# Making 22 contexts' keys and values one layer early, in a decoder of four layers

## The chip, the cores and the metric

One core of a Trainium2 chip runs the kernel. The metric is the device time of one launch in microseconds (us), the median of several runs. TensorE (PE) multiplies matrices and turns tiles over, writing to PSUM; VectorE (DVE), ScalarE (ACT) and GpSimd (POOL) work on vectors; SyncE (SP) issues most of the transfers between DRAM and SBUF. Each engine runs its own instructions in order and waits for others on semaphores.

## The reference

The input x is 32 sequences of 32 tokens of 256 numbers; the context is 32 sets of 257 rows of 256. Four layers follow each other, and each has a cross attention to the context, a self attention and a feed-forward part, all added to x. What the change touches most is the cross attention of layer 1, with 16 query heads of 64 and a single head of keys and values:

```
xn = layer_norm(x, ln_g, ln_b)
cn = layer_norm(context, cln_g, cln_b)
q = (xn @ Wq) in 16 heads * scale
k, v = halves of cn @ Wkv               # one head, 64 + 64 wide
sim = einsum('bhid,bjd->bhij', q, k)
out = einsum('bhij,bjd->bhid', softmax(sim), v) @ Wo
h, gate = halves of xn @ Wff1
out = out + silu(gate) * h @ Wff2
```

Layer 0's feed-forward part, which stands before it, sends each token to the nearest of 8 experts, `a * silu(g) @ down[e]` with `a, g` the halves of `xn @ up[e]`.

## The kernel before

x stays in SBUF (`core.X`, 8 tiles of 128 tokens). Each part of a layer is a function with one block per engine, and the order of instructions on each engine is written out by hand. Two areas `core.weights[0]` and `[1]` hold a part's weights in turn; `load_weights` fills the next layer's while one works (`pack3` are the weights of layer 1's cross attention, `pack4` those of its self attention).

*Layer 0's experts* (`l0_feed_forward`): POOL scales the rows (L2115), PE and DVE find each token's expert (`router_tensor`, `ex.places`), SP stores the rows in DRAM and loads three experts. Then POOL adds the skip part to X (L2119) and issues gathers of sorted rows (L1062 in `move_rows`). PE runs filler matmuls (`keep_busy`, L91) while it waits: 10 before the tokens are found, 8 before the first gather has landed, 28 behind the loop over 15 groups. `up` is L1113, `down` L1124.

*Layer 1's cross attention* (`l1_cross`): the context's mean and spread come from tiles that SP loads in four slots (`ContextNorm.load`), with DVE taking statistics (L1391, L1396). The layer norm of the context is folded in: the weights get cln_g and lose their mean (`scaled_kv`, `centred_kv`: L2272 on POOL, L2287 on PE, L2482 on DVE), and each context's keys and values are scaled with its spread afterwards. PE makes queries (L2302), the feed-forward's up (L2323) and down (L2384), and then turns over 32 contexts:

- `sim(b+1)`: scores of the next context, L2349, in PSUM banks 0 to 3. The odd heads' keys come from a copy in the other 64 partitions (`kT_odd`), which SP moves.
- `flip_probs(b)`: weights turned over, L2360.
- `keys_values(b+3)`: L2332, reads `ctxT` from DRAM; to bank 6.
- `weigh(b)`: L2376, reads the copied flipped weights.
- `flip_values(b+3)`: L2338, reads `kvT`.

DVE in one turn: tops of b+1 (L2519), its half of the copy of flipped weights of b (L2530), reciprocal of the first half's sums (L2524), `scale_keys_values(b+3)` (L2505, PSUM times the row of spreads), second reciprocal, `copy_values(b+3)` (L2513). ACT: its half of the copy (L2456), four exponentials (L2448), output copy (L2461). POOL multiplies the weights with the reciprocals (L2278), twice a turn.

At each border the norm of X follows: `take` gathers statistics of a pair of tiles, `early_vector` and `early_scalar` norm the first half of the tiles while the rest is being made, and PE flips them (L308).

Of the kernel before, what the change touches and what calls it, by code (L numbers as in the profile page):

```python
# [18 lines left out]
P = 128  # L19
# [15 lines left out]
class Core:  # L35


    def __init__(self, nc, es, dram):
# [33 lines left out]
        self.left = self.sem("left")  # L72
        self.norm = Norm(self)
# [84 lines left out]

def load_weights(core, sp, layer):

    w, mem = core.dram[f"pack{layer}"], core.weights[layer % 2]
    at = after_slots(layer)
    sp.dma_start(mem[:, at:at + w.shape[1]], w).then_inc(core.weights_in[layer], 16)
# [31 lines left out]
class Norm:  # L195
# [11 lines left out]
    def take(self, dve, written, tiles):  # L207

        c, nc = self.core, self.core.nc
        if written is not None:  # L210
            c.dve_step(dve, written)
        for t in tiles:
            done = nc.vector.bn_stats(c.stats[:, t, :], c.X[:, t, :])
# [142 lines left out]
class SelfAttention:  # L356
# [77 lines left out]
    def project_tensor(self, pe, xT, wqk, wv):  # L434
# [3 lines left out]
        self.project(pe, xT, xT, wqk, wv, (0, 1))  # L438
        flip.tensor(pe, 1)
        self.project(pe, xT, xT, wqk, wv, (2, 3))  # L440
# [31 lines left out]
    def copy_projections(self, act, side_of, squares=None, size=None, second_half=None, values_from=0, **root):  # L472
# [7 lines left out]
        for t in range(NT):  # L480
# [12 lines left out]
            if t == 1 and second_half is not None:  # L493
                second_half()
# [415 lines left out]
RING = 3  # L910

# [10 lines left out]
class SortedExperts:  # L922
# [10 lines left out]
    def __init__(self, core, es, name, layer, kind, choices, shared=False):  # L933
# [33 lines left out]
        if shared:  # L967
            self.slots = [sb("slot0", [P, width + extra])[:], mem[:, width:2 * width + extra], sb("slot2", [P, width + extra])[:]]
        else:
            whole = width + extra  # L970
            self.slots = [sb("slot0", [P, whole])[:], mem[:, whole:2 * whole], mem[:, 0:whole]]
# [81 lines left out]
    def move_rows(self, pool):  # L1053
# [17 lines left out]
        for i in range(RING):  # L1071
            gather(i)
        pool.wait_ge(places.targets_found, 1)
# [135 lines left out]
    def vector(self, dve, between=lambda n: None, final=False):  # L1209
# [51 lines left out]
        self.over(dve, lambda: None, turn, lambda: copy_out(*divmod(self.N - 1, RING), False), steps=4 if self.kind == "swiglu" else 0)  # L1261
        for g in range(NT // 2):
# [10 lines left out]
            else:  # L1273
                self.core.norm.take(dve, done, tiles)
                if g == 2:
                    self.core.norm.early_vector(dve)
# [171 lines left out]
def l0_cross(core, load_next):  # L1448
# [22 lines left out]
    with ExitStack() as es:  # L1471
# [95 lines left out]
        def _(pe):  # L1567
# [174 lines left out]
            core.keep_busy(0, 4)  # L1742

        @block.scalar
        def _(act):
# [115 lines left out]
            norm.roots(act, 0, 0)  # L1861
            out_squares(3, 7)
            norm.rows_by_scalar(act, 0, 0)

        @block.vector
        def _(dve):
# [148 lines left out]
            for pair, bank in enumerate((2, 3, 6, 7)):  # L2015
                norm.take(dve, add_out(pair, bank), (2 * pair, 2 * pair + 1))
                if pair == 2:
                    norm.early_vector(dve)


def l0_self(core, load_next):
# [5 lines left out]
    with ExitStack() as es:  # L2027
# [9 lines left out]
        def _(sp):  # L2037
            core.enter(sp)
            load_next(sp)

        @block.tensor
        def _(pe):
            flip.tensor(pe, 0, idle=(4, 2, 2))
# [21 lines left out]
        def _(dve):  # L2065
# [4 lines left out]
            for t in range(NT + 1):  # L2070
# [4 lines left out]
                if t == 1:  # L2075
# [7 lines left out]
def l0_feed_forward(core, load_next):  # L2083
# [5 lines left out]
    with ExitStack() as es:  # L2089
        ex = SortedExperts(core, es, "l0f", 2, "glu", 1)  # L2090
# [9 lines left out]
        gate_done = core.sem("l0f_gate_done")  # L2100
        block = core.block

        @block.sync
        def _(sp):
            core.enter(sp)
            load_next(sp)
# [3 lines left out]
        def _(pool):  # L2110
            pool.wait_ge(core.weights_in[2], 16)
# [5 lines left out]
            pool.wait_ge(skips_done, 1)  # L2117
            for t in range(NT):
                done = nc.gpsimd.tensor_scalar(core.X[:, t, :], core.X[:, t, :], more[:, t:t + 1], less[:, t:t + 1], ALU.mult, ALU.add)  # L2119
            done.then_inc(skipped, 1)  # L2120
            ex.move_rows(pool)

        @block.tensor
        def _(pe):
            flip.tensor(pe, 0, idle=(4, 1, 2))
            flip.tensor(pe, 1, idle=(4, 0, 3))
            core.enter(pe)
            pe.wait_ge(dist_ready, 1)
            for c in range(C):
                nc.tensor.matmul(PS[:, 4, NT * E:NT * E + E], ones[:], cent2[:, c, :], start=(c == 0), stop=(c == 1))  # L2130
            router_tensor(core, pe, XT, centm2, dist_done)
            ex.places.tensor(pe, gate, gate_done)
            core.keep_busy(7, 10)
            ex.places.find_tensor(pe, ex.gathered)
            core.keep_busy(7, 8)
            ex.tensor(pe, XT)
            core.keep_busy(0, 28)

        @block.scalar
        def _(act):  # L2140
# [9 lines left out]
            nc.scalar.activation(size[:], core.moments[:, :, 1], ACT.Sqrt, bias=core.eps5).then_inc(rooted, 1)  # L2150
            ex.scalar(act)
            norm.load_table(act)
# [2071 lines left out]
```

## Time and profile before

| | |
|---|---|
| runs | 1919.78, 1925.15, 1927.46 us; median 1925.15 |
| profiled execution | 1924.18 us, span 1922.4 us |
| PE busy | 1807.1 us, 94% of the span |
| DVE, ACT, POOL busy | 1057.6, 835.4, 552.3 us |
| PE in the chain that ended last | 79% |
| layer 0's experts | 247 to 384 us, loop from 286.9 to 371.9 |
| layer 1's cross attention | 384 to 685 us, loop over contexts from 515.1 to 664.3 |

The shares of busy time are means over stages with different limits, so single stages are read by their own timelines. The granted clock (PEclk) is TensorE's, as a share of 2.4 GHz.

### The profile page before, as it was taken

The page shows a single profiled execution, that of the slowest core. Times are in us where ns is not written, and L with a number is a line of the kernel's source. Part 1 is how long each engine was busy: PE and PEld are TensorE (multiplying, and loading weights), DVE is VectorE, ACT ScalarE, POOL GpSimd, SP SyncE. Part 2 cuts the span into 40 slices and gives each one's busy share as a digit, 9 for nine tenths or more (in the row PEclk, how much of TensorE's full clock was granted, in tenths as well). Part 3 has the DMA queues.
Part 4 walks back from the last instruction along what each step waited for, and adds up shares of the span by engine and source line. Part 5 has one row for each costly group of instructions (what it writes and reads, how often), then busy time and mean ns, then how long its engine had stood idle before and what let it go on. Part 6 is the DMA issues. An engine that isn't in the chain of part 4 may idle for free.

```text
span 1922.4 us, 43109 instructions
## 1 busy us (share of the span) xinstructions
PE 1807.1 (94%) x16872; PEld 1403.4 (73%) x16872; DVE 1057.6 (55%) x2665; ACT 835.4 (43%) x2389; POOL 552.3 (29%) x596
## 2 busy tenths in 40 slices
PE   8999879999999999899999989999789899998898
PEld 6887559944777756699999967777654477766787
DVE  7787741262366437866555545556665555447411
ACT  6665521132256444333333335555521566636332
POOL 4440133200144302211222113332212456515142
PEclk9999979999999999999999999999899999999899
DMA  4220068671144110042899733210111355300397
GB/s 150 57 57 5 2 241 284 206 226 46 49 101 104 42 56 3 3 160 82 300 333 335 286 109 108 51 46 26 44 56 59 100 154 157 108 1 2 111 350 260
DMA packets 87008, 233.91 MB, mean 122 GB/s; under 512 B 9776, under 2 KB 45136, under 8 KB 80304
## 3 DMA queue, kind: packets, MB, share of 16 engines
q1 hardware_dynamic: 78992, 213.90, 33.8%
q0 software_dynamic: 5664, 15.47, 2.4%
q8 instruction: 121, 1.98, 0.4%
q10 hardware_dynamic: 2176, 2.10, 0.3%
q14 instruction: 55, 0.45, 0.1%
HBM read 216.21 MB, written 12.07 MB: 119 GB/s over the span
## 4 chain that ended last, share of the span: by engine, by line
PE 79%; DVE 9%; issue 4%; ACT 3%; DMA 3%; POOL 2%; ACTq 0%; SPq 0%; POOLq 0%; PEldq 0%; DVEq 0%; PEld 0%
PE PS L1113 15%; PE PS L1582 6%; PE PS L1124 5%; PE PS L3594 3%; PE PS L3097 3%; PE PS L3619 3%; PE PS L3415 3%; PE PS L3105 3%; PE PS L2323 3%; PE PS L2672 2%; PE PS L2349 2%; PE PS L2376 2%; PE PS L2360 2%; PE PS L3130 2%; PE PS L2384 1%
## 5 line engine op out<-in xcount | busy, mean ns | idle before, releaser
L2278 POOL TENSOR_TENSOR l1x_probs<-l1x_probs,l1x_total 128x512 f32<-128x512 f32 x64 | 65.1, 1038 | 204.5 <-DVE l1x_total L2524 204.5
L1582 PE MATMUL PS<-weights,l0x_ctxT 128*128 128x256 f32 x512 | 120.7, 386 | 0.0
L1113 PE MATMUL PS<-l1f_xT,l1f_slot 128*128 128x128 f32 x1024 | 117.0, 275 | 0.0
L1113 PEld LDWEIGHTS PS<-l1f_xT,l1f_slot 128*128 128x128 f32 x1024 | 115.7, 192 | 0.1
L1582 PEld LDWEIGHTS PS<-weights,l0x_ctxT 128*128 128x128 f32 x512 | 94.4, 190 | 14.6 <-issue 2.1
L91 PE MATMUL PS<-consts 128*128 128x256 f32 x402 | 102.4, 404 | 1.2
L3067 POOL TENSOR_TENSOR l2x_probs<-l2x_probs,l2x_total 128x512 f32<-128x512 f32 x64 | 65.0, 1038 | 128.0 <-DVE l2x_total L3263 128.0
L91 PEld LDWEIGHTS PS<-consts 128*128 128x128 f32 x402 | 78.8, 203 | 14.8 <-issue 4.2
L1240 DVE SCALAR_TENSOR_TENSOR l1f_product<-PS,l1f_slot,l1f_side 128x128 f32<-128x128 f32 x128 | 36.0, 344 | 65.9 <-ACT l1f_side L1196 55.2
L3594 PE MATMUL PS<-l3x_keysT,l3x_QW 128*128 128x289 f32 x256 | 67.7, 407 | 1.7 <-issue 1.7
L1067 POOL DMA_INDIRECT l1f_out_dram<-l1f_out,l1f_sort_target_row x23 | 22.7, 985 | 159.5 <-DVE l1f_out L1223 159.5
L1196 ACT ACTIVATE l1f_side<-PS,l1f_slot 128x128 f32<-128x128 f32 x128 | 36.5, 368 | 66.0 <-PE PS L1113 62.9
L1762 ACT ACTIVATE l0x_sq<-PS 128x256 f32<-128x256 f32 x128 | 47.8, 385 | 32.9 <-PE PS L1582 32.9
L1113 PE MATMUL PS<-HT,weights 128*128 128x128 f32 x512 | 61.2, 282 | 0.9 <-DVE l1f_gated L1245 0.7
L1113 PEld LDWEIGHTS PS<-HT,weights 128*128 128x128 f32 x512 | 60.4, 198 | 1.7 <-DVE l1f_gated L1245 1.1
L3619 PE MATMUL PS<-tagged,l3x_QT 128*128 128x256 f32 x256 | 60.6, 379 | 0.9 <-ACT tagged L3715 0.9
L3097 PE MATMUL PS<-l2x_ctxT,weights 128*128 128x257 f32 x256 | 61.1, 381 | 0.0
L2323 PE MATMUL PS<-HT,weights 128*128 128x512 f32 x128 | 58.6, 619 | 2.2 <-DVE l1x_AT L2488 2.2
L1240 DVE SCALAR_TENSOR_TENSOR l1f_product<-PS,weights,l1f_side 128x128 f32<-128x128 f32 x120 | 33.8, 345 | 48.8 <-ACT l1f_side L1196 46.4
L3105 PE MATMUL PS<-weights,l2x_ctxT 128*128 128x256 f32 x256 | 60.4, 379 | 0.0
L3205 ACT ACTIVATE l2x_probs<-PS,l2x_top 128x257 f32<-128x257 f32 x128 | 59.2, 482 | 1.3 <-DVE l2x_top L3257 1.3
L1196 ACT ACTIVATE l1f_side<-PS,weights 128x128 f32<-128x128 f32 x120 | 34.2, 367 | 58.4 <-PE PS L1113 58.4
(661 smaller groups left out, 4590.7 us busy)
## 6 DMA issues: line engine op xcount, KB each, us to landing
l1f_slot<-in_experts_up_dram SPq DMA_DIRECT2D x16, 2056.0 KB
weights<-in_experts_up_dram SPq DMA_DIRECT2D x8, 2056.0 KB, 8.3
weights<-in_experts_down_dram SPq DMA_DIRECT2D x21, 640.0 KB, 4.5
weights<-in_experts_up_dram SPq DMA_DIRECT2D x10, 1024.0 KB
l1f_slot<-in_experts_down_dram SPq DMA_DIRECT2D x16, 640.0 KB, 4.4
l0x_ctxT<-in_ctxT_dram SPq DMA_DIRECT2D x32, 257.0 KB, 2.7
l1x_ctxT<-in_ctxT_dram SPq DMA_DIRECT2D x32, 257.0 KB
l2x_ctxT<-in_ctxT_dram SPq DMA_DIRECT2D x32, 257.0 KB, 2.7
```

The costliest lines, as they stand in the source:

```text
L91: self.nc.tensor.matmul(self.PS[:, bank, 0:2 * P], self.ident, self.consts[:, 0:2 * P], start=True, stop=True)
L1113: done = nc.tensor.matmul(PS[:, bank + a, m * P:(m + 1) * P], mat[:, c, m * P:(m + 1) * P], x, start=(c == 0), stop=(c == 1))
L1124: done = nc.tensor.matmul(PS[:, 7, 0:D], self.hidden[j][:, m, :], w["down"][:, m, :], start=(m == 0), stop=(m == 3))
L1196: nc.scalar.activation(self.side[u][:, m, :], PS[:, 2 * u, m * P:(m + 1) * P], ACT.Identity, bias=w["b1"][:, 4 * u + m:4 * u + m + 1]).the ...
L1240: done = nc.vector.scalar_tensor_tensor(p[:, m, :], PS[:, 2 * u + 1, m * P:(m + 1) * P], w["b3"][:, 4 * u + m:4 * u + m + 1], self.side[u] ...
L1582: last = nc.tensor.matmul(PS[:, 2 * (b % 2) + k, half * D:(half + 1) * D], ctxT[b % SLOTS][:, c, half * P:(half + 1) * P], kw[:, c, k * D: ...
L2278: nc.gpsimd.tensor_tensor(p, p, bcast(total[b % 2][:, 2 * n:2 * n + 2], 2, KEYS), ALU.mult).then_inc(probs_done, 1)
L2323: done = nc.tensor.matmul(PS[:, 2 * (n % 2) + g, :], ff1[:, c, (g * HB + m) * P:(g * HB + m + 1) * P], core.HT[:, c, half * 512:(half + 1) ...
L3097: last = nc.tensor.matmul(PS[:, 4 + 2 * o, 0:CTX], wk[:, c, o * P:(o + 1) * P], ctxT[b % 2][:, c, :], start=(c == 0), stop=(c == 1))
L3105: last = nc.tensor.matmul(PS[:, 5, half * D:(half + 1) * D], ctxT[b % 2][:, c, half * P:(half + 1) * P], wv[:, c, :], start=(c == 0), stop ...
L3594: done = nc.tensor.matmul(PS[:, 2 * (b % 2) + u, 0:KEYS], QW[:, c, b, 4 * u:4 * u + 4, :].rearrange("p h q -> p (h q)"), keysT[b % 2][:, c ...
L3619: nc.tensor.matmul(PS[:, 6 + c, 0:2 * P], tokens[b % 2][:, half, c * P:(c + 1) * P], probsT[b % 2][:, half, :], start=(half == 0), stop=False)
```

## The change

1. `l1_cross` finds 22 contexts' keys and values (`AHEAD`) made already, in `core.ahead`, a part of `weights[0]`. They are made in `l0_feed_forward` where PE ran fillers: 2 behind the router, 7 instead of `keep_busy(7, 10)`, 6 instead of `keep_busy(7, 8)`, 7 behind the expert loop, where `keep_busy(0, 28)` becomes `keep_busy(0, 14)`. ACT copies each from PSUM to SBUF and issues 13 of the context loads; the first 9 are loaded in `l0_self`. The scaling and centring of the keys/values weights moves there too, ahead of POOL's row scaling. The experts of layer 0 get slots of their own in SBUF.
2. `pack3` is loaded in two pieces in layer 0; its columns 5870 to 10496 (feed-forward weights, 2313 KB) come first on SP's queue in `l1_cross`, ahead of the context tiles. `pack4` (2628 KB) is loaded in six parts within the loop.
3. POOL issues gathers 0 to 2 of layer 0's experts before the skip work.
4. In the loop of `l1_cross` scores are made two contexts ahead, in halves, and the keys/values matmul stands before `flip_probs`, for contexts 22 to 31 alone. DVE's order is changed with it, and its scaling reads SBUF for contexts 0 to 21.
5. `early_vector` goes ahead of the statistics of the pair in several parts (and with it `early_scalar` in `l0_cross`), some fillers at the borders are fewer, and in the self attentions of layers 0 and 2 the second half's flips come one tile later.

```diff
 # l0_feed_forward, TensorE; project_ahead(batches) makes centred_kv x ctxT[b] in PSUM for each b
+            project_ahead(range(AHEAD_BY_PART[0]))
             ex.places.tensor(pe, gate, gate_done)
-            core.keep_busy(7, 10)
+            project_ahead(range(AHEAD_BY_PART[0], HEAD - AHEAD_BY_PART[2]))
             ex.places.find_tensor(pe, ex.gathered)
-            core.keep_busy(7, 8)
+            project_ahead(range(HEAD - AHEAD_BY_PART[2], HEAD))
+            pe.wait_ge(ahead_kept, HEAD)
             ex.tensor(pe, XT)
-            core.keep_busy(0, 28)
+            project_ahead(range(HEAD, AHEAD))
+            core.keep_busy(0, 14)
 # ScalarE
+            def keep_ahead(batches):
+                for b in batches:
+                    act.wait_ge(ahead_done, b + 1)
+                    n = b + AHEAD_SLOTS
+                    if n < AHEAD:
+                        act.dma_start(core.ahead_slots[b % AHEAD_SLOTS], core.dram["ctxT"][n]).then_inc(again_in if n < HEAD else late_in, 16)
+                    nc.scalar.copy(core.ahead[:, b, :], PS[:, ahead_bank(b), 0:CTX]).then_inc(ahead_kept, 1)
 # move_rows, GpSimd
         for i in range(RING):
             gather(i)
+        between()
...
 # l1_cross, SyncE
             core.enter(sp)
+            sp.dma_start(core.weights[1][:, AHEAD_AT:10496], core.dram["pack3"][:, AHEAD_AT:10496]).then_inc(ff_in, 16)
             cn.load(sp, slots)
-            load_next(sp)
...
 # TensorE
+            sim(1, (0, 1))
             for b in range(B):
-                if b + 1 < B:
-                    sim(b + 1)
-                flip_probs(b)
+                if b + 2 < B:
+                    sim(b + 2, (0,))
                 if b + 3 < B:
                     keys_values(b + 3)
+                flip_probs(b)
+                if b + 2 < B:
+                    sim(b + 2, (1,))
...
 # VectorE
-                nc.vector.tensor_tensor(kvT[b % 2][:], PS[:, 6, 0:CTX], rstd[b % 2][:], ALU.mult).then_inc(kv_scaled, 1)
+                nc.vector.tensor_tensor(kvT[b % 2][:], core.ahead[:, b, :] if b < AHEAD else PS[:, 6, 0:CTX], rstd[b % 2][:], ALU.mult).then_inc(kv_scaled, 1)
...
             for b in range(B):
-                if b + 1 < B:
-                    tops(b + 1)
+                if b + 3 < AHEAD:
+                    scale_keys_values(b + 3)
+                if b + 2 < B:
+                    tops(b + 2, (0,))
+                if AHEAD <= b + 3 < B:
+                    scale_keys_values(b + 3)
                 copy_probs(b)
-                if b + 1 < B:
-                    weights(b + 1, 0)
-                if b + 3 < B:
-                    scale_keys_values(b + 3)
-                if b + 1 < B:
-                    weights(b + 1, 1)
+                if b + 2 < B:
+                    tops(b + 2, (1,))
+                    weights(b + 2, 0)
                 if b + 3 < B:
                     copy_values(b + 3)
+                if b + 2 < B:
+                    weights(b + 2, 1)
```

## Rows read from the trace of the kernel before

**Rows 1.** The page, part 4: the chain of waits, share by engine.

```profile
PE 79%; DVE 9%; issue 4%; ACT 3%; DMA 3%; POOL 2%; ACTq 0%; SPq 0%; POOLq 0%; PEldq 0%; DVEq 0%; PEld 0%
```

**Rows 2.** Table by stage: stretch, length, busy and instructions per engine, PEclk, DMA share, GB/s.

```profile
260.00:267.00 7.00, 5.07 (x18) 4.32 (x18) 4.46 (x15) 0.00 (x0) 0.00 (x0) 0.51 0.89 315
441.00:447.00 6.00, 5.20 (x6) 2.19 (x7) 1.31 (x3) 0.00 (x0) 0.00 (x0) 0.50 0.21 55
515.00:653.00 138.00, 132.85 (x1144) 98.33 (x1142) 90.65 (x210) 83.84 (x300) 60.52 (x60) 1.00 0.40 96
1356.00:1376.00 20.00, 14.21 (x80) 10.82 (x78) 18.20 (x57) 6.84 (x18) 0.00 (x0) 1.00 0.00 0
```

**Rows 3.** Timeline of TensorE, one turn: start, length, line, out<-in, count.

```profile
565.25 0.48 PE L2349 MATMUL PS<-l1x_kvT,l1x_QT 64*128 64x257 f32 x1
...
566.32 1.09 PE L2360 MATMUL PS<-consts,l1x_probs 128*128 128x128 f32 x8
...
567.25 1.03 PE L2332 MATMUL PS<-l1x_ctxT,l1x_centred_kv 128*128 128x257 f32 x4
...
568.39 1.09 PE L2376 MATMUL PS<-l1x_probsT,l1x_V 128*64 128x128 f32 x16
...
569.43 0.44 PE L2338 MATMUL PS<-consts,l1x_kvT 128*128 128x128 f32 x2
...
569.80 0.48 PE L2349 MATMUL PS<-l1x_kvT,l1x_QT 64*128 64x257 f32 x1
```

**Rows 4.** Timeline of VectorE, then GpSimd, in the same turn.

```profile
564.22 0.17 DVE L2524 RECIPROCAL l1x_total<-l1x_total 128x2 f32<-128x2 f32 x1 [0.63 <-ACT l1x_probs L2448]
...
564.40 0.43 DVE L2505 TENSOR_TENSOR l1x_kvT<-PS,l1x_rstd 128x257 f32<-128x257 f32 x1
...
567.45 0.69 DVE L2530 COPY l1x_probsT<-PS 128x512 f32<-128x512 f32 x1 [0.15 <-PE PS L2360]
...
564.47 2.03 POOL L2278 TENSOR_TENSOR l1x_probs<-l1x_probs,l1x_total 128x512 f32<-128x512 f32 x2 [2.52 <-DVE l1x_total L2524]
```

**Rows 5.** Timeline of GpSimd, layer 0's experts.

```profile
275.06 4.30 POOL L2119 TENSOR_SCALAR X<-X,l0f_more,l0f_less 128x256 f32<-128x256 f32 x8 [17.65 <-DVE l0f_more L2186]
```

**Rows 6.** Timeline of TensorE, start of layer 0's expert loop.

```profile
285.26 0.69 PE L1093 MATMUL PS<-consts,l0f_rows_in 128*128 128x128 f32 x2 [6.76 <-DMA l0f_rows_in<-l0f_rows_dram,l0f_sort_token_row]
...
286.89 5.59 PE L1113 MATMUL PS<-l0f_xT,l0f_slot 128*128 128x128 f32 x32
```

**Rows 7.** Timeline of TensorE, behind that expert loop.

```profile
371.91 12.25 PE L91 MATMUL PS<-consts 128*128 128x256 f32 x56
```

**Rows 8.** TensorE, then VectorE, early in layer 1's cross attention.

```profile
388.62 0.68 PE L2287 MATMUL PS<-l1x_scaled_kv,l1x_mean_of 128*128 128x128 f32 x4 [0.18 <-POOL l1x_scaled_kv L2272]
...
428.62 0.69 DVE L2488 TENSOR_TENSOR l1x_AT<-PS,tagged 128x512 f32<-128x512 f32 x1 [1.43 <-ACT tagged L2442]
```

**Rows 9.** DMA issues of the page: count, KB, median us to landing.

```profile
weights<-in_pack_dram SPq DMA_DIRECT2D x1, 2564.0 KB, 9.3
```

**Rows 10.** Timeline of TensorE, second wait of the feed-forward up.

```profile
441.80 10.09 PE L2323 MATMUL PS<-HT,weights 128*128 128x512 f32 x16 [2.23 <-DVE l1x_AT L2488]
```

**Rows 11.** Timeline of TensorE, before the loop and at its end.

```profile
514.76 0.44 PE L2338 MATMUL PS<-consts,l1x_kvT 128*128 128x128 f32 x2 [0.52 <-DVE l1x_kvT L2505]
...
652.22 0.45 PE L2349 MATMUL PS<-l1x_kvT,l1x_QT 64*128 64x257 f32 x1 [0.30 <-ACT l1x_probs L2448]
```

**Rows 12.** Timeline of VectorE, end of layer 2's cross attention.

```profile
1339.87 0.75 DVE L213 BATCH_NORM_STATS2 stats<-X 128x6 f32<-128x256 f32 x2
```

**Rows 13.** Line L3972 in all; one on VectorE; GpSimd at that time.

```profile
L3972 DVE TENSOR_TENSOR l3a_V<-l3a_V,l3a_gates x8: 426/998/1003, 1732.9 to 1755.8; 128x256 f32<-128x256 f32 x8
...
1732.88 0.99 DVE L3972 TENSOR_TENSOR l3a_V<-l3a_V,l3a_gates 128x256 f32<-128x256 f32 x1
...
1732.33 1.27 POOL L3920 TENSOR_TENSOR l3a_products<-l3a_QK,weights 128x512 f32<-128x512 f32 x1 [1.23 <-DVE l3a_QK L3965]
```

**Rows 14.** Timeline of GpSimd, layer 3's cross attention.

```profile
1565.66 0.51 POOL L3842 TENSOR_TENSOR l3x_QT<-l3x_QT,l3x_total 128x66 f32<-128x66 f32 x1 [1.92 <-DVE l3x_total L3773]
```

More of the change, by code:

```diff
@@ L72, in __init__ @@
         self.left = self.sem("left")
+        self.ahead_in = self.sem("ahead_in")
+        self.ahead = self.weights[0][:, 0:AHEAD * CTX].rearrange("p (b k) -> p b k", k=CTX)
+        self.centred_kv = self.weights[0][:, AHEAD * CTX:AHEAD * CTX + C * P].rearrange("p (c n) -> p c n", c=C)
+        self.ahead_slots = [self.weights[1][:, AHEAD_AT + i * C * CTX:AHEAD_AT + (i + 1) * C * CTX].rearrange("p (c k) -> p c k", c=C) for i in range(AHEAD_SLOTS)]
         self.norm = Norm(self)
@@ L156, in take, with load_part @@
         return out
+def load_part(core, sp, layer, part, parts):
+    w, mem = core.dram[f"pack{layer}"], core.weights[layer % 2]
+    at, n = after_slots(layer), (w.shape[1] + parts - 1) // parts
+    columns = slice(part * n, min((part + 1) * n, w.shape[1]))
+    sp.dma_start(mem[:, at + columns.start:at + columns.stop], w[:, columns]).then_inc(core.weights_in[layer], 16)
 def load_weights(core, sp, layer):
@@ L205, in __init__, with take @@
         self.rows_dve = core.sem("norm_rows_dve")
-    def take(self, dve, written, tiles):
+    def take(self, dve, written, tiles, early=False):
         c, nc = self.core, self.core.nc
@@ L211, in take @@
             c.dve_step(dve, written)
+        if early:
+            self.early_vector(dve)
         for t in tiles:
@@ L1273, in vector @@
             else:
-                self.core.norm.take(dve, done, tiles)
-                if g == 2:
-                    self.core.norm.early_vector(dve)
+                self.core.norm.take(dve, done, tiles, early=(g == 2))
 def first_best(core, dve, values, number, best, place, chosen):
@@ L2039, in _ @@
             load_next(sp)
+            for b in range(AHEAD_SLOTS):
+                sp.dma_start(core.ahead_slots[b], core.dram["ctxT"][b]).then_inc(core.ahead_in, 16)
         @block.tensor
         def _(pe):
-            flip.tensor(pe, 0, idle=(4, 2, 2))
+            flip.tensor(pe, 0, idle=(4, 0, 2))
             pe.wait_ge(core.weights_in[1], 16)
@@ L2547, in add_out @@
                 written = nc.vector.tensor_tensor(x, PS[:, out_bank(first), at:at + n * D].rearrange("p (t d) -> p t d", t=n), x, ALU.add)
-                norm.take(dve, written, tiles)
+                norm.take(dve, written, tiles, early=(tiles == (4, 5)))
             for t in range(NT - 1):
```

195 lines of the change are left out of this document (121 added, 74 removed).

## The prediction, made before the changed kernel was run

> **What bounds the kernel now.** The page's chain of waits comes first: 79% of it is TensorE (PE) [rows 1]. A step moved on another engine pays only where PE waits for it, and a matmul taken off PE only where PE doesn't wait anyway. The table by stage [rows 2] gives the loop over contexts of layer 1's cross attention: PE works 132.85 of 138 us, at full clock. Two of its other rows, 260 to 267 and 441 to 447, were granted about half. Then the timelines show single steps.
>
> One turn of the loop takes 4.55 us: scores start at 565.25 and again at 569.80 [rows 3]. Scores take 1.07, `flip_probs` starts at 566.32, the keys/values matmul at 567.25, `weigh` at 568.39, `flip_values` at 569.43. From `flip_probs` to `weigh` it is 2.07: DVE's copy of the flipped half starts 1.13 behind the flip, at 567.45, and `weigh` 0.94 behind the copy [rows 4]. PE's own work there is 0.93 for the flip and 0.86 for keys/values (its row's 1.03 less the 0.17 by which a next matmul overlaps it), 1.79 in all. So the keys/values matmul lies almost wholly under DVE's copy, and that decides much below.
>
> **Experts of layer 0.** POOL's skip work takes 4.30 from 275.06 [rows 5]; the first gathers follow it, at about 279.5. Their rows reach PE at 285.26, after 6.76 us of idle, and the first up starts at 286.89 with 5.59 for 32 matmuls [rows 6]. The change puts gathers 0 to 2 ahead of the skip work: 4.3 earlier. The fillers before it become real matmuls of 0.86 a context: two where PE idled behind the router, seven (6.0) for ten fillers, six (5.2) for eight (a filler or a matmul in these rows counts as two records); at full clock this is what the fillers took, at half clock 12 and 10. Of the up's 5.59 about a third goes if the clock is full by then; I take a third of that, 0.6. ACT's copies pass beside PE. Thirteen reloads of 257 KB on ACT's queue compete with the expert weights, where DMA is at 0.89 already [rows 2], so a gather may take longer than the 5.7 us that it took. Behind the experts seven contexts (6.0) and 14 fillers (half of 12.25 [rows 7]) are as long as 28 fillers were. POOL's scaling of the keys/values weights, with its two small loads, stands ahead of the rows that it prepares for the experts; nobody reads these before the gathers. **-4.9**, bounds -9 (full clock, nothing late) and +1 (fillers at half clock reach past the gather).
>
> **Start of layer 1's cross attention.** The mean matmuls (0.68) go from PE [rows 8], and the norm's early order takes the statistics of a pair off the way to the flips (0.75 [rows 12] and about 0.2 to aggregate them): -1.65 where all of it counts. Against it, 2313 KB of feed-forward weights now lead the context tiles on SP's queue (2564 KB took 9.3 [rows 9]), which puts DVE's statistics some 2.1 later. In the turns around 428.62 DVE waited 1.43 for ACT [rows 8]; three such waits take up most of that before DVE releases PE at 441.80, where PE had idled 2.23 and was then granted half [rows 2, 10]. **-1.0**, bounds -1.9 and +1.
>
> **Feed-forward down.** Three keys/values matmuls leave. Two stood between PE-bound matmuls, 0.86 each. The third ended the phase: `flip_values` waited for DVE until 514.76 [rows 11]; now DVE scales right behind its last addition, 0.43 sooner. **-2.15**, bounds -2.6 and -1.2.
>
> **The loop.** Nineteen turns (b up to 18, and 29) have no keys/values matmul. PE's ring there is half of the scores 0.54, `flip_probs` to `weigh` 2.07 (still DVE's copy), `weigh` 1.03, `flip_values` 0.37: 4.01. The other half of the scores takes the place of the keys/values matmul, so only this half leaves the ring: -0.54 x 19 = -10.2. Ten late turns carry the matmul in front of `flip_probs`, where nothing covers it: 4.01 + 0.86 = 4.87, +0.32 x 10 = +3.2. In the first turn DVE has the tops and reciprocals of context 1, a scale and the first tops of context 2 ahead of its copy; from scores(1) at 515.13 through the four exponentials (0.45 each) I come to a copy at 519.65 and `weigh` at 520.6, not 518.3: +2.3. At the end scores(31), 1.07 with 0.30 of idle before them, no longer stand between two projections [rows 11]: -1.4. **-6.1**. Bounds: -9 (0.15 a turn more, if `weigh` follows the copy sooner) and +10 (the rival below). POOL and ACT leave the ring, since scores are two contexts ahead. The odd keys' copy (64 KB) has a turn to land. The 2628 KB for layer 4, in six parts beside late turns with DMA at 0.40 [rows 2], cost nothing; with no cover a part (438 KB, a sixth of 9.7) would hold an odd copy by 1.6, within its turn.
>
> DVE's own order in an early turn, from the start of `weigh`: values copied at 1.5, second reciprocal 1.8, scale 2.0, first tops 2.4 to 3.0; its copy can start at 1.03 + 0.37 + 0.54 + 1.13 = 3.07. DVE has under 0.1 to spare.
>
> **Norm orders at the other borders.** Between layer 2's cross and self attention the early vector work stood behind statistics of 0.75 and 0.2 [rows 12]; it goes ahead, and the chain over ACT's rows and the flips is 0.9 shorter. By the same reading -0.8 after layer 1's experts and -0.4 before layer 3's self attention. Before layer 3's cross attention it is -1.6, of which I give 1.3 back: four fillers leave, PE idles about 2.5, and an idle of 2.23 was followed by half clock [rows 2, 10]. After layer 0's cross attention ACT's rows come early but DVE copies the head only behind its last statistics, 0.3 later since ACT's squares moved back, and PE idles about 3: +2.0 (0.3 to 3.6). Sum **-0.4**, bounds -3.5 and +5.
>
> **Sum**: -4.9 - 1.0 - 2.15 - 6.1 - 0.4 = -14.55. The profiled execution took 1924.18 (span 1922.4), 0.97 under the median of 1925.15: 1909.6, rounded to 1910.
>
> **Rivals.** *DVE held by POOL (R2).* The scale of an early turn reads two SBUF tensors, where it read PSUM and one. Such a DVE instruction, `l3a_V` of 128x256, took 0.43 at its shortest and 1.00 at the median; a long one began at 1732.88 while POOL ran from 1732.33 to 1733.60, and ended 0.27 behind it [rows 13]. The other way round, POOL's multiply of 66 columns behind a DVE instruction that had begun was drawn out to 0.51 [rows 14]. In the new order the scale stands right behind the reciprocal that also releases POOL's multiply of 1.04. In before DVE followed this reciprocal by 0.18 (564.22 to 564.40), POOL by 0.25 (564.47) [rows 4], so DVE should be first, by 0.07. If POOL is, the scale ends 0.25 + 1.04 + 0.27 = 1.56 behind the reciprocal and not 0.61: 0.95, less the spare 0.1, in 19 turns +16. Total 1926.
> The Trainium skill ("SBUF — State Buffer", section Who interferes with whom) says that a DVE instruction with two SBUF inputs contends with a GpSimd instruction that reads SBUF, and that whichever was issued first blocks the other for its whole length. By that rule the trace agrees in both orders, 1.00 against 0.43; a turn is 4.0 if DVE is issued first and 4.86 if POOL is.
> *Gather no sooner (R3).* It queues behind expert weights and reloads: the experts give +1, not -4.9; 1915.5. DMA at 0.89 speaks for it; against it, POOL's queue is its own and its rows are few beside 4.6 MB of experts.
> *Half clock in the loop (R1), slower than before.* An early turn holds 1.07 + 0.93 + 1.03 + 0.37 = 3.40 of PE work in 4.01 (0.85); it was 132.85 of 138 (0.96). At 1.2 GHz the work doubles to 6.8, 2.8 more than forecast each turn. It decides from six such turns (14.55 / 2.8 = 5.2); all nineteen give 1963. Against it: a turn's longest idle is 0.6, and 1356 to 1376, with 14.21 busy of 20, stayed at 1.00 [rows 2].
> *Half clock behind every border.* +5 and not -0.4: 1915.
>
> **How the numbers follow.** Forecast 0.56 (own range 1902 to 1915); R2 0.20; R3 0.10; borders 0.10; R1 0.04. 0.5% (9.6 us) is about what a measurement can tell from no change: faster is under 1915.5, slower over 1934.8. Faster: 0.56, half of R3 and borders (0.10), 0.02 of R2 where the rest comes out well: 0.68. Slower: R1 0.04 and 0.02 of R2 on top of bad borders: 0.06. Same 0.26. The range goes down to 1900 (experts at -9 and turns at 3.86 together lie at 1902.6) and up to 1926 (R2).
>
> **What would show it.** Turns 4.0 apart early and 4.9 late; `l1x_kvT` at 0.43 (R2: 1.0 or more, turns 4.8); the experts' first up near 282.3 (R3: 286); `flip_values` of context 2 right behind the last addition; a granted clock of 1.00 in the loop (R1: 0.5). The prediction is wrong if the scale is stretched, if loads push the gathers, or if half clock follows the idles at the borders.

## The result, and the profile after the change

| | before | after |
|---|---|---|
| median of 20 runs each | 1923.5 us | 1916.1 us |
| ratio of times, 95% interval | | 0.9966 [0.9955, 0.9978] |
| profiled execution (span) | 1924.18 (1922.4) us | 1916.3 (1914.5) us |

The change gains about 6.5 us by the ratio (1923.5 x 0.0034), 7.4 by the medians, and 7.9 between the two profiled executions, where 14.55 were forecast. The ratio is that of fast runs alone: one run of the changed kernel took 4822 us, the other 19 took 1910.5 to 1922.1. The time lies inside the range of 1900 to 1926, but the gain is about half of the forecast and below the 0.5% that was called faster.

In the chain of waits PE's share is 75%, from 79% [rows 1]. The table by stage after the change has the columns of [rows 2]; here the stretches are the first turn and the loop.

```profile
502.00:516.00 14.00, 10.70 (x51) 7.14 (x50) 7.35 (x16) 6.55 (x22) 4.25 (x4) 0.79 0.13 29
516.00:656.00 140.00, 129.61 (x1110) 90.99 (x1110) 85.42 (x207) 87.11 (x300) 64.14 (x60) 1.00 0.29 74
```

The loop ran at full clock (1.00), as it did in [rows 2], so the rival R1 is out. The new thing is the stretch from 502 to 516: PE busy 10.70 of 14 and a granted clock of 0.79, where before had 1.00 throughout (502 to 516, and 515 to 653 in [rows 2]).

**Experts.** TensorE's timeline after, up to the first up:

```profile
273.88 7.14 PE L2189 MATMUL PS<-weights 128*128 128x257 f32 x24
281.88 0.41 PE L1117 MATMUL PS<-consts,l0f_rows_in 128*128 128x128 f32 x2 [0.86 <-DMA l0f_rows_in<-l0f_rows_dram,l0f_sort_token_row]
283.71 0.41 PE L1117 MATMUL PS<-consts,l0f_rows_in 128*128 128x128 f32 x2 [1.41 <-DMA l0f_rows_in<-l0f_rows_dram,l0f_sort_token_row]
283.95 5.36 PE L1137 MATMUL PS<-l0f_xT,l0f_slot 128*128 128x128 f32 x32
```

The matmuls for six contexts (24 records, four to a context) end only 0.86 before the first rows arrive, where PE idled 6.76 [rows 6]. They take 7.14 and not the 5.2 of the forecast; the granted clock from 272 to 281 was 0.81. The first up starts at 283.95, not at 286.89: 2.9 earlier, not 4.6 as forecast (282.3), and not as late as R3 has it (286). It takes 5.36, not 5.59.

**Start of the cross attention.** TensorE after, the first two waits of the feed-forward up:

```profile
422.71 14.00 PE L2402 MATMUL PS<-HT,weights 128*128 128x512 f32 x32 [3.08 <-DVE l1x_AT L2572]
...
440.27 7.13 PE L2402 MATMUL PS<-HT,weights 128*128 128x512 f32 x16 [2.23 <-DVE l1x_AT L2572]
```

The first wait is new. The second has the same length (2.23) as that in [rows 10], but the 16 matmuls behind it took 7.13 at full clock instead of 10.09. VectorE after has its own wait for a context tile ahead of the statistics:

```profile
393.41 2.87 DVE L1415 BATCH_NORM_STATS2 l1x_ctx_stats<-l1x_probsT 128x256 f32 x8 [3.77 <-DMA l1x_probsT<-in_ctx_dram]
```

**First turn.** TensorE before, scores(0) and `weigh(0)`:

```profile
508.58 0.48 PE L2349 MATMUL PS<-l1x_kvT,l1x_QT 64*128 64x257 f32 x1 [0.30 <-DVE X L2540]
...
518.28 1.09 PE L2376 MATMUL PS<-l1x_probsT,l1x_V 128*64 128x128 f32 x16
```

TensorE after, from scores(0) to `weigh(0)`, and then VectorE:

```profile
502.36 0.48 PE L2432 MATMUL PS<-l1x_kvT,l1x_QT 64*128 64x257 f32 x1 [0.30 <-DVE X L2625]
...
508.85 0.44 PE L2420 MATMUL PS<-consts,l1x_kvT 128*128 128x128 f32 x2 [1.71 <-DVE l1x_kvT L2590]
...
511.87 0.76 PE L2432 MATMUL PS<-l1x_kvT,l1x_QT 64*128 64x257 f32 x1 [1.30 <-ACT l1x_probs L2534]
...
513.03 1.97 PE L2443 MATMUL PS<-consts,l1x_probs 128*128 128x128 f32 x8
...
516.08 1.45 PE L2459 MATMUL PS<-l1x_probsT,l1x_V 128*64 128x128 f32 x16
```

```profile
507.55 1.25 DVE L2590 TENSOR_TENSOR l1x_kvT<-weights,l1x_rstd 128x257 f32<-128x257 f32 x1
```

PE waits 1.71 for `kvT` of context 2, which took DVE 1.25 instead of 0.43 [rows 4], then 1.30 for ACT; `flip_probs` then takes 1.97 and `weigh` 1.45, where a turn at full clock has 1.09 for each. In before, `weigh(0)` stood 9.70 behind scores(0); here it is 13.72. The table by half microseconds shows where the clock fell, to half and ahead of the second wait:

```profile
510.00:510.50 0.50, 0.50 (x4) 0.00 (x0) 0.50 (x1) 0.00 (x0) 0.00 (x0) 0.52 0.51 115
```

In the half microsecond before it the clock was 1.00.

**A turn.** TensorE after, an early turn (b up to 18):

```profile
521.57 0.44 PE L2420 MATMUL PS<-consts,l1x_kvT 128*128 128x128 f32 x2
521.94 0.48 PE L2432 MATMUL PS<-l1x_kvT,l1x_QT 64*128 64x257 f32 x1
...
522.57 1.09 PE L2443 MATMUL PS<-consts,l1x_probs 128*128 128x128 f32 x8
...
524.65 1.09 PE L2459 MATMUL PS<-l1x_probsT,l1x_V 128*64 128x128 f32 x16 [0.35 <-DVE l1x_probsT L2615]
525.68 0.44 PE L2420 MATMUL PS<-consts,l1x_kvT 128*128 128x128 f32 x2
```

VectorE and GpSimd in another early turn:

```profile
563.44 0.15 DVE L2609 RECIPROCAL l1x_total<-l1x_total 128x2 f32<-128x2 f32 x1
563.51 0.41 DVE L2590 TENSOR_TENSOR l1x_kvT<-weights,l1x_rstd 128x257 f32<-128x257 f32 x1
...
564.89 0.69 DVE L2615 COPY l1x_probsT<-PS 128x512 f32<-128x512 f32 x1 [0.32 <-PE PS L2443]
```

```profile
563.68 1.14 POOL L2361 TENSOR_TENSOR l1x_probs<-l1x_probs,l1x_total 128x512 f32<-128x512 f32 x1 [0.28 <-DVE l1x_total L2609]
```

TensorE in a late turn (b from 19):

```profile
612.69 1.14 PE L2412 MATMUL PS<-l1x_ctxT,weights 128*128 128x257 f32 x4
613.66 1.03 PE L2443 MATMUL PS<-consts,l1x_probs 128*128 128x128 f32 x8
...
615.68 1.09 PE L2459 MATMUL PS<-l1x_probsT,l1x_V 128*64 128x128 f32 x16 [0.35 <-DVE l1x_probsT L2615]
```

An early turn is 4.11 (521.57 to 525.68), forecast 4.01; a late one 5.03, forecast 4.87; before it was 4.55 [rows 3]. `kvT` starts 0.07 behind the reciprocal and takes 0.41, POOL follows at 0.24 and takes 1.14 instead of 1.04. So DVE is first, as forecast, and R2 doesn't decide the loop. It decides one instruction outside it, the 1.25 at 507.55.

### The profile page after: what moved, and what is told of

The parts are those of the page before. It is cut to its first block, busy times and chain, and to the rows that moved or that the text cites. A ratio compares the mean times of both kernels' runs of the same rounds, so it can differ in the third digit from the quotient of the medians.

```text
span 1914.5 us, 42986 instructions
## 1 busy us (share of the span) xinstructions
PE 1792.7 (94%) x16790; PEld 1384.6 (72%) x16790; DVE 1049.4 (55%) x2665; ACT 847.6 (44%) x2411; POOL 555.5 (29%) x596
## 3 DMA queue, kind: packets, MB, share of 16 engines
q8 instruction: 120, 1.97, 0.4%
## 4 chain that ended last, share of the span: by engine, by line
PE 75%; DVE 11%; DMA 5%; issue 4%; ACT 3%; POOL 1%; SPq 0%; ACTq 0%; POOLq 0%; PEldq 0%; DVEq 0%; PEld 0%
PE PS L1137 15%; PE PS L1606 6%; PE PS L1148 5%; PE PS L3682 3%; PE PS L3502 3%; PE PS L3186 3%; PE PS L3707 3%; PE PS L3194 3%; PE PS L2402 2%; PE PS L2459 2%; PE PS L2761 2%; PE PS L2443 2%; PE PS L3219 2%; DMA l1x_probsT<-in_ctx_dram 2%; PE PS L2473 1%
## 5 line engine op out<-in xcount | busy, mean ns | idle before, releaser
L95 PE MATMUL PS<-consts 128*128 128x256 f32 x320 | 81.8, 401 | 1.2
L95 PEld LDWEIGHTS PS<-consts 128*128 128x128 f32 x320 | 61.7, 201 | 12.3 <-issue 4.4
L2534 ACT ACTIVATE l1x_probs<-PS,l1x_top 128x257 f32<-128x257 f32 x128 | 59.8, 475 | 6.8 <-DVE l1x_top L2604 4.4
## 6 DMA issues: line engine op xcount, KB each, us to landing
weights<-in_experts_up_dram SPq DMA_DIRECT2D x8, 2056.0 KB, 10.2
```

What stands on the lines that cost most here:

```text
L95: self.nc.tensor.matmul(self.PS[:, bank, 0:2 * P], self.ident, self.consts[:, 0:2 * P], start=True, stop=True)
```

## The experiments

Each is compared with the kernel before on the same chip. A turn is the distance of two `weigh`. All but the ninth and tenth start from the changed kernel or from one that an earlier experiment built on it.

**First: scores behind the flip.** The prediction's sum kept half of the scores in PE's ring. This experiment takes them out: both halves stand under DVE's copy.

```diff
-                if b + 2 < B:
-                    sim(b + 2, (0,))
-                if b + 3 < B:
-                    keys_values(b + 3)
                 flip_probs(b)
+                if b + 3 < B:
+                    keys_values(b + 3)
                 if b + 2 < B:
-                    sim(b + 2, (1,))
+                    sim(b + 2, (0, 1))
 # VectorE: copy_probs(b) first, then the scale of late turns, tops(b + 2, (0, 1)), weights
```

> The changed kernel, with both halves of the scores behind flip_probs (and, in late turns, behind the keys/values matmul), DVE's copy ahead of all tops. Theory (ring): what stands between flip_values and flip_probs lengthens the turn, what stands between flip_probs and weigh is covered by DVE's copy (2.07). Early turns fall from 4.10 to 3.5 if only this ring counts, to 3.8 if DVE's scale ahead of its copy holds it; late turns from 5.03 to 4.35. About -11 against the changed kernel: 1905. Rival (a vector engine already needs 4.1 a turn, PE's order does nothing): turns stay at 4.1, total 1916.

Measured 1901.68 us against 1921.68, ratio 0.9899 [0.9872, 0.9927]. Its early turns are 3.91, its late ones 4.21. TensorE, then VectorE, in an early turn:

```profile
565.94 1.09 PE L2459 MATMUL PS<-l1x_probsT,l1x_V 128*64 128x128 f32 x16 [0.51 <-DVE l1x_probsT L2613]
```

```profile
564.54 0.54 DVE L2588 TENSOR_TENSOR l1x_kvT<-weights,l1x_rstd 128x257 f32<-128x257 f32 x1
565.00 0.68 DVE L2613 COPY l1x_probsT<-PS 128x512 f32<-128x512 f32 x1
```

PE's wait in front of `weigh` is still there (0.51), now because DVE's scale, drawn out to 0.54, stands ahead of its copy. (POOL's first multiply began at 563.76; with its usual 1.04 it ends at 564.80, and the scale at 565.08, 0.28 behind it.) In late turns, where the copy stands first, everything on PE is back to back. Against the change (0.9966) this is another 0.7% for two groups of matmuls moved, twice what the whole change brings.

**Second: `kvT` of context 2 sooner.** DVE's scale goes ahead of the weights of context 0, where POOL is idle.

```diff
             tops(0, (0, 1))
+            scale_keys_values(2)
             for n in range(2):
                 weights(0, n)
             add_feed_forward(NT - 1)
-            scale_keys_values(2)
```

> The changed kernel, with DVE's scale of context 2 ahead of the weights of context 0, so that POOL isn't multiplying then. Theory: its 1.25 us falls to 0.41, flip_values of context 2 starts right behind the last feed-forward matmul (-1.7), and TensorE's half clock of the first turn goes: weigh(0) at 512 to 513 instead of 516.08, total -3.5. Rival (the half clock comes from the 1.3 us wait for exponentials alone, or stays): -1.7 or less.

Measured 1911.89 against 1921.68, 0.9941 [0.9921, 0.9961]. TensorE:

```profile
512.16 1.09 PE L2443 MATMUL PS<-consts,l1x_probs 128*128 128x128 f32 x8
...
514.43 1.09 PE L2459 MATMUL PS<-l1x_probsT,l1x_V 128*64 128x128 f32 x16 [0.54 <-DVE l1x_probsT L2615]
```

From scores(0) at 503.95, `weigh(0)` now takes 10.48 and not 13.72: 3.24 less, close to the 3.5 expected. Against the change (0.9966 [0.9955, 0.9978]) the two intervals overlap a little. Without the first idle (1.71) the second (1.51 here) was followed by full clock, and the flip takes 1.09 again.

**Third: a small instruction between reciprocal and scale,** to let POOL begin first.

```diff
+                if 3 <= b < AHEAD:
+                    nc.vector.memset(spare[:], 0.0)
```

> The changed kernel, with one DVE memset of 128x1 ahead of the scale in the 19 early turns; it computes nothing that is used. Theory (a port that DVE and POOL share goes to whoever is first): the scale now starts behind POOL's multiply and ends with it, 1.1 to 1.2 instead of 0.41, the turn goes from 4.10 to 4.8, total +13: 1929. Rival (POOL and DVE don't hold each other): only the memset's own 0.1 a turn, +2: 1918.

Measured 1913.61 against 1921.68, 0.996 [0.9946, 0.9974], the same as the change. VectorE:

```profile
561.98 0.42 DVE L2593 TENSOR_TENSOR l1x_kvT<-weights,l1x_rstd 128x257 f32<-128x257 f32 x1
562.00 0.06 DVE L2586 MEMSET l1x_spare<- 128x1 f32 x1
```

The scale still starts 0.08 behind the start of the reciprocal (561.90); the memset's record lies beside it. POOL wasn't put first, so this says nothing on R2.

**Fourth: the skip work ahead of the gathers again.**

```diff
+        between()
         for i in range(RING):
             gather(i)
-        between()
```

> The changed kernel, with POOL's skip work ahead of the first three gathers again, as before the change. Theory (the gathers' issue sets the first up): first up at 287 to 288 instead of 283.95, +3.5 in all. Rival (the gathers wait in queues full of expert weights and context loads until about 284 either way): first up at 285 or less, +1.

One run took 1924.29. TensorE:

```profile
287.62 0.66 PE L1117 MATMUL PS<-consts,l0f_rows_in 128*128 128x128 f32 x2 [7.91 <-DMA l0f_rows_in<-l0f_rows_dram,l0f_sort_token_row]
...
289.64 5.58 PE L1137 MATMUL PS<-l0f_xT,l0f_slot 128*128 128x128 f32 x32
```

The first up is 5.7 later than in the change (3 to 4 expected) and 2.8 later than in before [rows 6]. POOL's skip work itself starts at 276.30 and not at 275.06 [rows 5], which is 1.2 of the 2.8. The first gather then takes 6.85 (280.77 to 287.62) where before took 5.73 (279.53 to 285.26), another 1.1. DMA was at 1.04 here as its rows landed (287 to 288) and at 0.08 there (285 to 286); this kernel has the reloads of the context in flight too, but no run takes them away. Without the gathers first, the matmuls made ahead would have cost this stage something.

**Fifth: the scale where POOL is idle.** On top of the first and second, each context's scale is done one turn sooner, between the tops and the first reciprocal.

```diff
                 if b + 2 < B:
                     tops(b + 2, (0, 1))
+                if b + 4 < AHEAD:
+                    scale_keys_values(b + 4)
                 if b + 2 < B:
                     weights(b + 2, 0)
 # and scale_keys_values(3) behind tops(1)
```

> The first and second experiment together (scores behind flip_probs, scale of context 2 first), and DVE's scale one context further ahead, between the tops and the first reciprocal, when POOL is idle. Theory: in the first experiment DVE's ring was copy 0.6, tops 1.28, exponentials 0.55, reciprocal and values, 0.55, reciprocal, scale 0.46 = 3.91; the scale moves into the wait for the exponentials, the turn is 3.5 (the ring of TensorE, 3.47), the scale 0.41. Late turns stay at 4.2. Total 1901.7 - 8 - 3 = 1890. Rival (DVE waits for something else there, the turn stays at 3.9): 1898.

Measured 1890.05 against 1920.01, 0.9842 [0.9818, 0.9867]: the best kernel of this study. Its turns are 3.43 early and 4.20 late. VectorE, and the group of all 22 scales (shortest, median and longest in ns):

```profile
558.40 0.42 DVE L2588 TENSOR_TENSOR l1x_kvT<-weights,l1x_rstd 128x257 f32<-128x257 f32 x1
```

```profile
L2588 DVE TENSOR_TENSOR l1x_kvT<-weights,l1x_rstd x22: 415/417/421, 485.9 to 572.1; 128x257 f32<-128x257 f32 x22
```

**Sixth: the same, but behind the first reciprocal.** Only the place of the scale differs: behind `weights(b + 2, 0)` and `copy_values(b + 3)`, when POOL is multiplying. This does what the third was meant to do.

```diff
-                if b + 4 < AHEAD:
-                    scale_keys_values(b + 4)
                 if b + 2 < B:
                     weights(b + 2, 0)
                 if b + 3 < B:
                     copy_values(b + 3)
+                if b + 4 < AHEAD:
+                    scale_keys_values(b + 4)
```

> As the one before, with the scale two instructions later in DVE's order: behind the first reciprocal and the values, ahead of the second reciprocal; DVE's sum of work is the same. Theory (POOL and DVE hold each other): POOL's multiply has begun 0.25 behind the first reciprocal, the scale starts at 0.3 and ends with it at 1.5: 1.2 instead of 0.41, and the second reciprocal is 0.6 late: turns of 4.0 to 4.1, total +10 against its neighbour. Rival (no holding): turns of 3.5 as in its neighbour, total the same.

Measured 1900.54 against 1920.01, 0.9896 [0.9872, 0.992]: 10.5 more than the fifth. VectorE, GpSimd and the group:

```profile
558.85 1.28 DVE L2588 TENSOR_TENSOR l1x_kvT<-weights,l1x_rstd 128x257 f32<-128x257 f32 x1
```

```profile
558.80 1.04 POOL L2361 TENSOR_TENSOR l1x_probs<-l1x_probs,l1x_total 128x512 f32<-128x512 f32 x1 [1.46 <-DVE l1x_total L2607]
```

```profile
L2588 DVE TENSOR_TENSOR l1x_kvT<-weights,l1x_rstd x22: 416/1276/1278, 486.4 to 582.7; 128x257 f32<-128x257 f32 x22
```

POOL began at 558.80, the scale at 558.85; POOL ended at 559.84, the scale at 560.13, after 1.28. The turn is 3.97 and not 3.43. So the mechanism of R2 is real: 0.86 on each scale, of which 0.54 reach the turn. The Trainium skill ("SBUF — State Buffer", section Who interferes with whom) has the instruction that was issued first block the other for its whole length; the two kernels agree with that, 1.28 against 0.42, and so does the 1.25 of the first turn. In the other order less than that is seen: POOL's record, begun 0.17 behind the scale, is 0.10 longer (1.14 for 1.04), while the scale had 0.24 left.

What lets POOL hold the scale is where its input lies. From PSUM the same instruction isn't held: in the ninth experiment (below) it starts within POOL's pair of multiplies and takes 0.43.

```profile
561.76 0.43 DVE L2507 TENSOR_TENSOR l1x_kvT<-PS,l1x_rstd 128x257 f32<-128x257 f32 x1
```

```profile
560.28 2.03 POOL L2278 TENSOR_TENSOR l1x_probs<-l1x_probs,l1x_total 128x512 f32<-128x512 f32 x2 [2.17 <-DVE l1x_total L2526]
```

So it was the change itself, by keeping the product in SBUF, that made the place of this instruction matter.

**Seventh: the feed-forward weights behind the first four slots of context tiles.**

```diff
-            sp.dma_start(core.weights[1][:, AHEAD_AT:10496], ...).then_inc(ff_in, 16)
-            cn.load(sp, slots)
+            cn.load(sp, slots, lambda: sp.dma_start(core.weights[1][:, AHEAD_AT:10496], ...).then_inc(ff_in, 16))
```

> The changed kernel, with the 2313 KB of feed-forward weights behind the first four context tiles on SP's queue. Theory (the load ahead of them delays the statistics, and with them the first hidden): DVE's statistics start at about 389.5 instead of 393.41, the wait of 3.08 for the first hidden at 422.71 goes. Rival (DMA's rate over the whole 40 us sets it: the same bytes lie ahead of the last tile): statistics start sooner, wait later, and the 3.08 stays within 1.

One run took 1917.1. VectorE:

```profile
390.24 2.70 DVE L1416 BATCH_NORM_STATS2 l1x_ctx_stats<-l1x_probsT 128x256 f32 x8
399.21 2.88 DVE L1416 BATCH_NORM_STATS2 l1x_ctx_stats<-l1x_probsT 128x256 f32 x8 [6.28 <-DMA l1x_probsT<-in_ctx_dram]
```

The statistics start at once, at 390.24, and then wait 6.28 for the fifth tile. PE's wait in the feed-forward up is 2.81 where the change has 3.08. Order on the queue only moves the wait, as the rival has it. What sets it isn't shown: DMA's share between 396 and 424 was 0.66 to 0.80, so the transfers weren't at their fullest, and the four slots of the tiles weren't varied.

**Eighth and eleventh: the borders of before.** The order of norms, fillers and flips at all borders as before, in the changed kernel and in the fifth.

```diff
-                norm.take(dve, written, tiles, early=(tiles == (4, 5)))
+                norm.take(dve, written, tiles)
+                if tiles == (4, 5):
+                    norm.early_vector(dve)
 # and so at the other borders; keep_busy(0, 2) is 4 and keep_busy(0, 1) is 5 again
```

> The changed kernel, with all norm orders, fillers and flip places at the borders of the layers as they were before the change. Theory (they gave next to nothing: what came early was waited for by the next engine, or cost a half clock): total the same as the changed kernel within 2 us: 1916 to 1918; 1.5 us slower right behind layer 1's experts, faster by as much in layer 0's and layer 2's self attention. Rival (they were worth the 3 to 4 us that the statistics of a pair take at each border): 1920.

> The fifth experiment with the norm orders, fillers and flip places of before at the borders. Theory (they are worth nothing within what can be measured, as in the eighth): 1889 to 1892. Rival (worth 3 or more, as the eighth's 0.9985 against 0.9966 could also be read): 1893 or more.

Eighth: 1916.95 against 1920.01, 0.9985 [0.9968, 1.0001], where the change has 0.9966. Eleventh: 0.984 [0.9811, 0.987], where the fifth has 0.9842. The intervals overlap in both, so no worth of the border orders is shown; the 3 to 4 us of the eighth's rival aren't excluded either (0.9985 less 0.9966 is 3.6 us).

The clock behind layer 0's cross attention (184 to 190 us) seems at first to speak against the new order: granted were 0.72 in the change and 1.00 in the eighth. But the eleventh, with the order of the eighth, had 0.77, and the first and fifth, with that of the change, had 1.00. So a cost in clock isn't shown either.

**Ninth: the order alone.** The kernel before, all keys and values made within the loop as before, with scores two contexts ahead behind `flip_probs` and the keys/values matmul.

```diff
+            sim(1)
             for b in range(B):
-                if b + 1 < B:
-                    sim(b + 1)
                 flip_probs(b)
                 if b + 3 < B:
                     keys_values(b + 3)
+                if b + 2 < B:
+                    sim(b + 2)
 # ScalarE, VectorE: exps and tops, weights of b + 2 where those of b + 1 stood
```

> The kernel before, with nothing made early: only the loop's order is that of the first experiment's late turns (scores two contexts ahead, behind flip_probs and the keys/values matmul). Theory (the order is worth as much by itself as the early keys and values are): all turns 4.2 instead of 4.55, 29 x 0.34 = 10 less, 1 to 2 given back in the first turn: 1912. Rival (without the early keys and values the order brings nothing, as in the changed kernel's late turns of 5.03): 1920 or more.

Measured 1915.72 against 1924.37, 0.9951 [0.993, 0.9971]. TensorE, one turn:

```profile
559.81 1.04 PE L2360 MATMUL PS<-consts,l1x_probs 128*128 128x128 f32 x8
560.68 1.03 PE L2332 MATMUL PS<-l1x_ctxT,l1x_centred_kv 128*128 128x257 f32 x4
561.65 0.48 PE L2349 MATMUL PS<-l1x_kvT,l1x_QT 64*128 64x257 f32 x1
...
561.97 0.38 PE L2349 MATMUL PS<-l1x_kvT,l1x_QT 64*128 64x257 f32 x1
...
562.40 0.38 PE L2349 MATMUL PS<-l1x_kvT,l1x_QT 64*128 64x257 f32 x1
...
562.72 1.10 PE L2376 MATMUL PS<-l1x_probsT,l1x_V 128*64 128x128 f32 x16
...
564.02 0.38 PE L2360 MATMUL PS<-consts,l1x_probs 128*128 128x128 f32 x2
```

The turn is 4.21 (559.81 to 564.02), back to back, and so are nearly all from the second on. A reordering that makes nothing ahead gains 0.49%, the change 0.34%; the intervals overlap. Where nothing waits, one keys/values matmul less saves 0.78 a turn (4.21 to the fifth's 3.43).

**Tenth: gathers first alone.** The kernel before with the gathers ahead of the skip work, and its fillers.

```diff
         for i in range(RING):
             gather(i)
+        between()
```

> The kernel before, with POOL's first three gathers ahead of its skip work and nothing else. Theory (the order of the gathers gives 5.7, the real work in place of fillers takes 2.8 of it back): first up at 281 to 282 instead of 286.89, total -5 to -6: 1915. Rival (the gathers alone can't land before the expert weights, at about 283.5; the work costs nothing): first up at 284, total -3.

Measured 1920.23 against 1924.37, 0.9987 [0.9968, 1.0006]. TensorE:

```profile
281.56 0.44 PE L1094 MATMUL PS<-consts,l0f_rows_in 128*128 128x128 f32 x2 [2.56 <-DMA l0f_rows_in<-l0f_rows_dram,l0f_sort_token_row]
284.02 0.66 PE L1094 MATMUL PS<-consts,l0f_rows_in 128*128 128x128 f32 x2 [2.02 <-DMA l0f_rows_in<-l0f_rows_dram,l0f_sort_token_row]
284.47 5.11 PE L1114 MATMUL PS<-l0f_xT,l0f_slot 128*128 128x128 f32 x32
```

The first up starts 2.4 sooner, not 5, although the first gather is issued 4.5 sooner (275.06 for 279.53): it takes 6.50 and not 5.73, and the second pair of rows comes 2.5 behind the first. The change has 2.9 of 4.2. The second rows come at 283.71 and 284.02 in the two kernels, with and without matmuls ahead: the landing of the gathers sets the first up, not PE's work in front of it.

## Why the prediction was wrong

The shift of the same PE step between the two profiled executions, in us, step by step:

| term | forecast | measured |
|---|---|---|
| experts of layer 0 | -4.9 | -3.2 |
| start of layer 1's cross attention | -1.0 | -1.3 |
| two keys/values pairs in the feed-forward down | -1.72 | -1.7 |
| first turn (third pair among it) | +1.9 | +4.0 |
| 19 early turns | -10.2 | -8.4 |
| 10 late turns | +3.2 | +4.8 |
| end of the loop | -1.4 | -1.5 |
| borders (measured: all behind the loop) | -0.4 | -0.5 |

The start of the cross attention runs from a shift of -3.2 behind the experts' first ups over -4.9 at the queries (the mean matmuls and the early norm: -1.7, as forecast) and -1.5 behind the new wait to -4.5 at the down. The measured terms sum to -7.8; the 0.1 to the 7.9 is rounding.

*Failed: the size of the loop.* Forecast -6.5 with the third pair in it, measured -1.1. Three terms of the sum:
- The first turn. "A copy at 519.65, `weigh` at 520.6" (in before's time) didn't count that DVE's scale of context 2 would find POOL multiplying context 0's weights (from 506.48, 2.03 for the two; the scale ends at 508.80, 0.29 behind them). The rival R2 was priced in the 19 turns alone, where DVE is first, and not at this one place, where POOL is. It cost 0.82 directly (1.25 for 0.43). In before the scale of the same context also started while POOL multiplied (514.28, POOL from 512.70 to 514.73), read PSUM and took its 0.43. Behind PE's idle of 1.71 the clock fell to half at 510.0. That was no accident of one execution: the profiles of the first, third, fourth, seventh and eighth experiments, which keep this scale where it was, all have half clock in the first turn, and those of the second, fifth, sixth and eleventh, which move it, have none. The second experiment gave 3.24 back by moving one instruction.
- The early turn, 4.11 for 4.01. The prediction took the spacing of rows in another order: `flip_values` to scores 0.37, half of the scores 0.54, the ring to `weigh` 2.07. Measured are 0.37, 0.63 (521.94 to 522.57), 2.08 and 1.03. So 0.09 of the 0.10 is the half of the scores. The ninth experiment's rows show why: of the four pairs of a whole group the first and the last take 0.32 each (561.65 to 561.97 and 562.40 to 562.72; the two between take 0.43). Cut in two, each half has a first and a last pair, 0.64, and not half of 1.07. 0.10 x 19 = 1.9.
- The late turn. The keys/values matmul costs 0.97 (612.69 to 613.66), and the turn 0.92 over an early one, where 0.86 was taken; with the 0.10 of the early turn that is the 0.16 x 10 = 1.6.

*Right: what bounds the turn.* Half of the scores leaves the ring, DVE's copy and its 0.3 wait for PE stay, POOL and ACT don't set it. The ring was read right and its use was not asked: the first and ninth experiments show that the rest of the scores could have left too.

*Experts: right in kind, 1.7 short.* The first gather is issued 4.2 sooner (275.32 for 279.53), of the 4.3 forecast. It takes 6.56 to land and not 5.73, so the first rows come 3.4 sooner; the second rows come 1.83 behind them, and the first up starts 2.9 sooner. The prediction named a longer landing and put nothing for it in the sum. The tenth gives 2.4 with fillers. The rest is the first up, 5.36 where 5.0 were forecast. R3 was put as all or nothing and lies between. That the experts' weights in flight hold the gathers fits with DMA at 0.98 from 272 to 281 and 1.01 from 281 to 290 in the change, but no run took these transfers away.

*Start of the cross attention: the number by luck.* The prediction had the statistics come 2.1 later and be swallowed by other waits. The load ahead of the tiles held them by 3.77, and DVE's first product stood at 421.98, where it was 421.75 in before, while PE had come 4.9 earlier. So a wait of 3.08 came ahead of PE's first hidden. Then 2.96 came back at the second wait, which kept its idle and not its half clock, and this isn't owed to the change. The fifth and sixth experiments have the same instructions up to the loop; here are their 16 matmuls behind this wait, in this order:

```profile
441.44 7.13 PE L2402 MATMUL PS<-HT,weights 128*128 128x512 f32 x16 [2.23 <-DVE l1x_AT L2570]
```

```profile
438.88 10.14 PE L2402 MATMUL PS<-HT,weights 128*128 128x512 f32 x16 [2.22 <-DVE l1x_AT L2570]
```

The ninth and tenth, which leave this part as it was before, have 7.13 and 7.13, and the first, second, third and eighth 8.56, 8.69, 8.62 and 8.82. The same idle is followed by full or half clock from one execution to the next. With 7.13 in before as well, the term would have been +1.7 and not -1.3. What decides between the two isn't shown.

*Borders: the sum says nothing.* Behind layer 0's cross attention PE was 2.8 late, 2.3 of it from this border, where +2.0 was forecast, but all of it was gone at the experts (256.75 us for 256.76), where PE had idled 1.54 at 252.50 in before. Behind the loop the shift goes from -7.4 to -10.9 in layer 1's experts (first rows), is -11.2 in layer 2's self attention, -10.0 in layer 3's cross attention, and comes back to -7.9 in the last expert loop. Most of these steps stand where nothing was edited; the tenth, edited in layer 0 alone, goes from -5.8 to -7.4 in layer 1's experts too. So the -0.5 that is left is a difference of larger steps, one profile of each kernel can't tell the border term, and its agreement with -0.4 is luck. The eighth and eleventh settle it no better.

*Rivals.* R1 didn't happen. R2 didn't happen in the loop: DVE followed the reciprocal by 0.07 and POOL by 0.24, the order read off [rows 4]. Where it was brought about, in the sixth, it cost 0.86 on the scale (1.28 less 0.42), near the 0.95 of the forecast, and 0.54 on the turn, in another order of DVE's instructions.

## What to carry to other kernels

In a ring of several engines, first name the wait that is covered and put all work of the waiting engine that has its inputs under it: the order alone brought 0.49%, and with it the work removed and the scale at its best place brought 1.6% (the fifth). A vector instruction that reads two tensors in SBUF belongs where GpSimd is idle; one at the wrong place in a loop cost 10 us, and a single one ahead of a loop 3. When a matmul leaves a place where another engine sets the time, price the ring that is left and not the matmul. When two profiles differ in clock at one place, look at the same place in kernels that the edit leaves alone, before the difference is put down to the edit.

## What was not expected of the hardware

- POOL's multiply, second behind the same reciprocal, is drawn out from 1.04 to 1.14 by the scale's 0.41; the scale, when second, from 0.42 to 1.28, ending 0.29 behind POOL.
- A memset of 128x1 has a record that begins 0.02 behind the scale that follows it in program order, and delays it by nothing.
- A scale of 128x257 from PSUM takes 0.43 within POOL's multiplies, the same from SBUF 1.25 to 1.28.
- An idle of 2.2 in the same place of the same instructions was followed by 16 matmuls in 7.13 in one execution and in 10.14 in another.
- A second set of gathered rows came 1.8 and 2.5 behind the first with the experts' weights in flight, and issuing the first gather 4.2 and 4.5 sooner brought 2.9 and 2.4.
